# Attention's results turned by VectorE in squares of 32 instead of by TensorE, with the division on GpSimd

## What is computed

```python
Q = (q_in @ wq + bq).reshape(Bq, Sq, H, HD)
Kp = (k_in @ wk + bk).reshape(Bq, Sk, H, HD)
V = (v_in @ wv + bv).reshape(Bq, Sk, H, HD)
scores = jnp.einsum('bqhd,bkhd->bhqk', Q, Kp) / jnp.sqrt(jnp.float32(HD))
# causal: scores above the diagonal are -inf
a = jax.nn.softmax(scores, axis=-1)
o = jnp.einsum('bhqk,bkhd->bqhd', a, V).reshape(Bq, Sq, Dm)
return o @ wo + bo

x = _layernorm(x + _attn(x, x, x, ..., True), ln1_g, ln1_b)
x = _layernorm(x + _attn(x, encoder_output, encoder_output, ..., False), ln2_g, ln2_b)
x = _layernorm(x + _moe(x, ...), ln3_g, ln3_b)
```

## Times and profile before

| | |
|---|---|
| median of 3 runs | 759.5 us (757.66 to 760.63) |
| profiled execution, span | 755.9 us |
| TensorE busy | 711.2 us, 94% |
| TensorE weight load busy | 478.4 us, 63% |
| VectorE busy | 499.0 us, 66% |
| ScalarE busy | 369.2 us, 49% |
| GpSimd busy | 287.3 us, 38% |

### The profile page before, as it was taken

One profiled execution on the slowest core, in us unless ns is written; L12 is line 12 of the kernel. 1 busy time (PEld: TensorE's weight loads), 2 busy tenths in 40 slices (PEclk: granted clock), 3 DMA queues, 4 the chain that ended last, 5 costly groups with the idle time before them and its releaser, 6 DMA issues.

```text
span 755.9 us, 14560 instructions
## 1 busy us (share of the span) xinstructions
PE 711.2 (94%) x4969; PEld 478.4 (63%) x4969; DVE 499.0 (66%) x1376; ACT 369.2 (49%) x749; POOL 287.3 (38%) x558
## 2 busy tenths in 40 slices
PE   6889999999999999999997889999999999999983
PEld 4444434545464454645563666898999999999941
DVE  5679788678766877756687744365666665666436
ACT  4325475665666676677753436433433332332403
POOL 8305521542653463624654333212332332232114
PEclk9999999999999999999997989999999999999997
DMA  8954431343164021316037762676999999999754
GB/s 273 291 145 128 114 98 46 84 129 128 34 179 127 13 60 48 92 43 179 14 113 237 223 210 95 204 262 226 357 328 343 343 326 341 343 332 333 236 187 163
DMA packets 95154, 140.29 MB, mean 186 GB/s; under 512 B 11855, under 2 KB 81077, under 8 KB 92597
## 3 DMA queue, kind: packets, MB, share of 16 engines
q1 hardware_dynamic: 76357, 107.86, 45.5%
q10 hardware_dynamic: 15072, 22.02, 9.1%
q0 software_dynamic: 3648, 9.45, 3.5%
HBM read 110.65 MB, written 28.65 MB: 184 GB/s over the span
## 4 chain that ended last, share of the span: by engine, by line
PE 75%; issue 8%; DVE 7%; DMA 5%; POOL 2%; ACT 1%; SPq 0%; DVEq 0%; ACTq 0%; POOLq 0%
PE out_acc L984 11%; PE score_pair L961 10%; PE work L932 9%; PE score_pair L855 8%; PE work L849 8%; PE work L906 6%; PE work L855 4%; PE score_pair L849 3%; PE work L1008 3%; DVE neg_part_max L1472 3%; PE work L918 2%; PE work L992 2%; PE work L935 2%; DMA arena<-parts_scratch 1%; PE out_acc L849 1%
## 5 line engine op out<-in xcount | busy, mean ns | idle before, releaser
L1472 DVE TENSOR_REDUCE neg_part_max<-work 128x1 f32<-128x512 f32 (+4 forms) x368 | 213.3, 625 | 70.4 <-PE work L935 35.9
L1244 ACT ACTIVATE arena<-score_pair 128x1024 f32<-128x1024 f32 (+2 forms) x224 | 178.9, 839 | 79.8 <-PE score_pair L961 78.9
L932 PE MATMUL work<-arena 96*128 96x77 bf16 (+4 forms) x640 | 118.5, 278 | 10.3 <-ACT arena L1207 2.7
L961 PE MATMUL score_pair<-arena 99*128 99x512 bf16 (+2 forms) x448 | 104.2, 337 | 4.0 <-DMA arena<-negmax_scratch 3.0
L984 PE MATMUL out_acc<-arena 128*32 128x512 f32 (+4 forms) x896 | 103.7, 517 | 2.6 <-DVE arena L1492 2.6
L1904 POOL DMA_INDIRECT chosen_scratch<-arena,scatter_rows x36 | 35.6, 989 | 176.5 <-DVE arena L1404 176.2
L855 PE MATMUL score_pair<-arena 128*128 128x256 f32 x432 | 97.6, 380 | 0.0
L932 PEld LDWEIGHTS work<-arena 96*128 96x128 bf16 x640 | 49.5, 99 | 74.5 <-issue 31.0
L1960 POOL TENSOR_SCALAR_AFFINE_SELECT arena<-arena 128x256 f32<-128x256 f32 x128 | 51.5, 410 | 117.9 <-ACT arena L1244 116.7
L1177 ACT ACTIVATE arena<-work,expert_b_cols 128x128 f32<-128x128 f32 x180 | 51.1, 369 | 77.3 <-PE work L849 64.0
L849 PE MATMUL work<-arena 128*128 128x128 f32 x720 | 87.7, 279 | 0.3 <-issue 0.3
(11 more groups left out here) (257 smaller groups left out, 955.0 us busy)
## 6 DMA issues: line engine op xcount, KB each, us to landing
arena<-in_L_xattn_e_w SPq DMA_DIRECT2D x54, 1024.0 KB, 7.1
arena<-parts_scratch SPq DMA_DIRECT2D x24, 768.0 KB, 6.1
arena<-in_L_xattn_e_w ACTq DMA_DIRECT2D x18, 1024.0 KB, 6.4
parts_scratch<-arena_more SPq DMA_DIRECT2D x24, 384.0 KB, 2.6
parts_scratch<-arena_more SPq DMA_DIRECT2D x24, 256.0 KB, 3.0
parts_scratch<-arena_more SPq DMA_DIRECT2D x24, 128.0 KB, 2.9
residual<-in_x SPq DMA_DIRECT2D x4, 512.0 KB, 8.1
tokens_scratch<-residual SPq DMA_DIRECT2D x2, 1024.0 KB, 5.4
```

The source lines that it names most:

```text
L932: m = pe.matmul(bank[:, j * it.w:(j + 1) * it.w], qa[st.half(it.g)][0:R_S, h, n0:n0 + P], k, start=True, stop=not it.last)
L961: m = pe.matmul(st2[pair][0:rows, j, 0:w], k, qa[st.half(it.g)][0:R_M, h, skip:QG], start=True, stop=True)
L1244: act_e.activation(pt[buf][0:rows, :, 0:w], st2[pair][0:rows, :, 0:w], ACT.Exp, scale=float(HD) ** -0.5).then_inc(pair_taken[pair], 1)
L1472: dve.tensor_reduce(pm[:, it.at, it.t, it.h0:it.h0 + it.nh], bank[:, 0:it.nh * it.w].rearrange("p (j k) -> p j k", j=it.nh), AX.X, ALU.max ...
```

## The change

The two turns on TensorE go. `normalise` is now always VectorE's: it turns `out_acc` in squares of 32x32 while it takes it out of PSUM. A head fills exactly one row of squares, so queries come to lie on partitions (32 of them, for each of 16 squares along the row) and the 32 values of a head along the row, its sum at place 16. VectorE takes the reciprocal of the 16 sums of each partition; `divide` is GpSimd's, a multiplication in SBUF. The quads now hold heads 0, 2, 4, 6 and 1, 3, 5, 7, and the second quad's 16 values are written beside the first quad's, in place of its ones. The new item `merge` (letter `t`) turns the 128x512 result back in squares, into `oT`, which has features on partitions and queries along the row, as `out_tile` needs it as stationary operand. `ot` has three buffers, `onT` is gone, `onat` becomes `oT`. `divide` and `out_turn` take no bank of `work` any more. In `ORDER` only `d` and `t` move: `d` stands close behind its `u` (before, several maxima lay between), `t` a few items behind the second `d` of a group, and the out_tiles stand in a row. All other letters keep their order. Three semaphores come new, three are joined with others.

```diff
-BANKED = ("xt", "ctx", "columns", "proj", "v", "v_bias", "max", "lay", "divide", "out_turn", "out_tile",
+BANKED = ("xt", "ctx", "columns", "proj", "v", "v_bias", "max", "lay", "out_tile",
@@ attend
         steps += [Item(kind, st=st, g=g, quad=quad) for kind in ("normalise", "divide")]
+        if quad == HH // QUAD - 1:
+            steps.append(Item("merge", st=st, g=g))
@@ ORDER, a stretch of self-attention and the end of the last stage
-    "upf2mlq2m3fmwqf2qfm3wqm3wfqsfm3gpdwmyrm2prslm5ruq2dm2qwm3q2m2wmqmqm3qmwmq2sfsm3fwqmqfm2wm2q2fwmqm2f2wfq2fm2q"
+    "lq2m3fmwqf2qfm3wqm3wfqsfm3gpwmyrm2prslm5ruqdqmtmqwm3q2m2wmqmqm3qmwmq2sfsm3fwqmqfm2wm2q2fwmqm2f2wfq2fm2qmwuqdm2qmw"
...
-    "udpdA3rpt2NADWsrNA2lU2so2lt2n3NBn4onUBhVYyUnonNZn3qnqnenha3U2YyR2wuZMaMq2dYR2qwAuq2M2AHNAwudqUwuUd2PZtNtotot"
-    "o2eU2YaZa3zNUYR2LRLRUZNKLSLCHUYPKSTUZNU2YUZUEOIA3XDY2Z2W"
+    "qMRMHyo2qzwuvdPKo2qSewuqdqFtq2BXwuadwax2Oa2xBkxIupdA2tArpNADWsrNA2lU2so2ln3NBn4onUBhVYyUnonNZn3qnqnenha3U2YyR2wuZd"
+    "MaMq2YR2qwAuqdqMtMAHNAwuqdUwuUdPZtNo4eU2YaZa3zNUYR2LRLRUZNKLSLCHUYPKSTUZNU2YUZUEOIA3XDY2Z2W"
@@ buffers
-        ot = [cut("arena", QG) for _ in range(2)]
+        ot = [cut("arena", QG) for _ in range(3)]
-        onat = [a.rearrange("p (t n) -> p t n", t=TB) for a in onat_words]
+        oT = [a.rearrange("p (c t) -> p c t", c=KC) for a in onat_words]
@@ where a quad is laid: the first of a group in ot[0] or ot[1], the second in ot[2]
+        def by_queries(it):
+            whole = ot[place_of[it.st.n, it.g]] if it.quad == 0 else ot[2]
+            return whole.rearrange("p (n v) -> p n v", v=SQUARE)
@@ tensor
-                        h = it.quad * QUAD + it.pair * 2 + j
+                        h = 2 * (it.pair * 2 + j) + it.quad
...
-                elif it.kind == "divide":
-                    e.wait_ge(o_taken, it.n + 1)
-                    o = ot[it.n % 2]
-                    for q in range(QT):
-                        m = pe.transpose(bank[:, q * P:(q + 1) * P], o[:, q * P:(q + 1) * P], ident[:, :])
-                    m.then_inc(full[it.bank], 1)
-
-                elif it.kind == "out_turn":
-                    last = divided[it.b, it.cross, it.t // QT]
-                    e.wait_ge(taken[last.bank], last.use)
-                    for c in range(KC):
-                        m = pe.transpose(bank[:, c * P:(c + 1) * P], onat[it.b][:, it.t, c * P:(c + 1) * P],
-                                         ident[:, :])
-                    m.then_inc(full[it.bank], 1)
-
                 elif it.kind == "out_tile":
-                    o = turned[it.cross, it.b, it.t]
-                    e.wait_ge(taken[o.bank], o.use)
+                    for n in stage_of[it.cross, it.b]:
+                        e.wait_ge(merged, merge_of[n, it.t // QT].n + 1)
@@ scalar: its half of normalise and its copy for out_turn go
-                    act_e.copy(ot[it.n % 2], o_ps[:, :]).then_inc(o_taken, 1)
...
-                    act_e.copy((onT if it.kind == "out_turn" else rT)[it.n % 2],
+                    act_e.copy(rT[it.n % 2],
@@ vector
-                elif it.kind == "normalise" and (it.g + it.quad) % 2 == 0:
+                elif it.kind == "normalise":
                     buf, use = prob_use(weigh_last[it.n], 1)
                     e.wait_ge(prob_taken[buf], use)
...
-                    dve.tensor_copy(ot[it.n % 2], o_ps[:, :]).then_inc(o_taken, 1)
...
+                    elif second_before[it.n]:
+                        e.wait_ge(divided, second_before[it.n].n + 1)
+                    dve.transpose(by_queries(it).rearrange("p n v -> p (n v)"), o_ps[:, :]).then_inc(o_taken, 1)
                     if it.n >= 2:
+                        e.wait_ge(divided, it.n - 1)
+                    e.wait_ge(o_taken, it.n + 1)
+                    dve.reciprocal(rsum[:, it.n % 2], by_queries(it)[:, :, HD]).then_inc(recip_ok, 1)
+
+                elif it.kind == "merge":
+                    for quad in range(HH // QUAD):
+                        e.wait_ge(divided, divide_of[st.n, it.g, quad].n + 1)
...
+                    dve.transpose(oT[st.b][:, st.hh, it.g * QG:(it.g + 1) * QG],
+                                  ot[place_of[st.n, it.g]]).then_inc(merged, 1)
@@ gpsimd
+                elif it.kind == "divide":
+                    e.wait_ge(recip_ok, it.n + 1)
+                    first = ot[place_of[st.n, it.g]].rearrange("p (n v) -> p n v", v=SQUARE)
+                    pool.tensor_tensor(first[:, :, it.quad * HD:(it.quad + 1) * HD], by_queries(it)[:, :, 0:HD],
+                                      rsum[:, it.n % 2].rearrange("p (n o) -> p n o", o=1).to_broadcast(
+                                          [P, QG // SQUARE, HD]), ALU.mult).then_inc(divided, 1)
```

More of the change, by code:

```diff
@@ L210, in project_out @@
     t0 = half * QT
-    tiles = [Item("out_turn", b=b, t=t0, cross=cross)]
-    for t in range(t0, t0 + QT):
-        if t + 1 < t0 + QT:
-            tiles.append(Item("out_turn", b=b, t=t + 1, cross=cross))
-        tiles.append(Item("out_tile", b=b, t=t, cross=cross))
+    tiles = [Item("out_tile", b=b, t=t, cross=cross) for t in range(t0, t0 + QT)]
     return tiles + [Item("out_scale", b=b, cross=cross, g=half)]
@@ L565, in build @@
         divides = find("divide")
-        turned = {(it.cross, it.b, it.t): it for it in find("out_turn")}
+        merges = find("merge")
+        merge_of = {(it.st.n, it.g): it for it in merges}
         tiled = find("out_tile")
@@ L577, in build @@
             pv_end_of_half[it.st.n, it.g] = it
-        for it in divides:
-            divided[it.st.b, it.st.cross, it.g] = it
-        out_read = {turned[it.cross, it.b, it.t].n: it for it in tiled}
+        tile_of = {(it.cross, it.b, it.t): it for it in tiled}
+        divide_of = {(it.st.n, it.g, it.quad): it for it in divides}
         r_turned = {(it.b, it.t): it for it in find("r_turn")}
@@ L584, in build @@
         ended = find("normalise")
+        place_of, merge_before, free, used_by = {}, {}, [0, 1], {}
+        for it in plan:
+            if it.kind == "normalise" and it.quad == 0:
+                a = place_of[it.st.n, it.g] = free.pop(0)
+                merge_before[it.st.n, it.g] = used_by.get(a)
+                used_by[a] = merge_of[it.st.n, it.g]
+            elif it.kind == "merge":
+                free.append(place_of[it.st.n, it.g])
+        second_before = {}
+        for n, it in enumerate([it for it in ended if it.quad == 1]):
+            second_before[it.n] = [z for z in ended if z.quad == 1][n - 1] if n else None
         weigh_last = [it for it in weighs if it.kb == it.st.blocks(it.g) - 1]
         stage_cross = {it.st.n: it.st.cross for it in weighs}
+        stage_of = {(c, b): sorted({it.st.n for it in weighs if (it.st.cross, it.st.b) == (c, b)})
+                    for c in (False, True) for b in range(B)}
         lays = find("lay")
@@ L739, in turn_read @@
         def turn_read(it):
-            it = (out_read if it.kind == "out_turn" else r_read)[it.n - 2]
+            it = r_read[it.n - 2]
             return (logit_sum, it.t % QT + 1) if it.kind == "r_mul_last" else (full[it.bank], it.use)
@@ L1245, in scalar @@
                                      scale=float(HD) ** -0.5).then_inc(pair_taken[pair], 1)
-                elif it.kind == "normalise" and (it.g + it.quad) % 2:
-                    buf, use = prob_use(weigh_last[it.n], 1)
-                    e.wait_ge(prob_taken[buf], use)
-                    if it.n >= 2:
-                        e.wait_ge(full[divides[it.n - 2].bank], divides[it.n - 2].use)
-                    else:
-                        e.wait_ge(full[columns.bank], columns.use)
-                        for z in ctx_of:
-                            e.wait_ge(full[z.bank], z.use)
-                    act_e.copy(ot[it.n % 2], o_ps[:, :]).then_inc(o_taken, 1)
-                elif it.kind in ("out_turn", "r_turn"):
+                elif it.kind == "r_turn":
                     e.wait_ge(full[it.bank], it.use)
@@ L1491, in vector @@
                             e.wait_ge(full[z.bank], z.use)
[L1492 to L1501 removed]
+                    elif second_before[it.n]:
+                        e.wait_ge(divided, second_before[it.n].n + 1)
+                    dve.transpose(by_queries(it).rearrange("p n v -> p (n v)"), o_ps[:, :]).then_inc(o_taken, 1)
+                    if it.n >= 2:
+                        e.wait_ge(divided, it.n - 1)
+                    e.wait_ge(o_taken, it.n + 1)
+                    dve.reciprocal(rsum[:, it.n % 2], by_queries(it)[:, :, HD]).then_inc(recip_ok, 1)
+                elif it.kind == "merge":
+                    for quad in range(HH // QUAD):
+                        e.wait_ge(divided, divide_of[st.n, it.g, quad].n + 1)
                     if st.cross:
[L1503 removed]
+                        z = tile_of[False, st.b, it.g * QT + QT - 1]
                         e.wait_ge(full[z.bank], z.use)
@@ L1610, in vector @@
                     if it.b == 0:
[L1612 removed]
```

(1 more changed line is left out.)

69 lines of the change are left out of this document (26 added, 43 removed), and 2 rows, old and new, of the table KINDS_OF_WORK.

## The result

The changed kernel takes 775.6 us (774.4 to 778.5), the kernel before, run beside it, 759.4 (757.7 to 760.6): a ratio of 1.0248, interval 1.0212 to 1.0283. (The quotient of the two medians alone is 1.0213, the lower end of that interval, so the loss is 16 to 19 us.) The prediction said 745.5, with 757 as its upper end. The profiled execution of the changed kernel has a span of 772.7 us, 16.8 more than before.

The account below looks back on a forecast made before the run. TensorE was taken to bound the kernel from 100 to 400 us. Gain 17.6 - 1 - 3 = 13.6, rounded to 14: span 755.9 to 742, plus 3.6 around it, 745.5 us; range 736 to 757.

Parts of the forecast that it names:

- the first rival: No new wait reaches TensorE and freed banks give back 3 us: gain 21, to 739, or 24, to 736; chance 0.15.
- the turn costs what the copy does: On VectorE, a 128x512 turn out of PSUM was priced at 0.70 us, by the 0.686 us copy.
- the price of the turns from 100 to 300 us: TensorE's removed divide and out_turn turns in that stretch: 7.0 us on the path, by the chain of waits.
- The third: VectorE's turn out of PSUM costs 1.63 us instead of 0.70, so the kernel is slower, 775 us; chance 0.07.
- The second: VectorE sets the pace: waiting merges delay maxima, TensorE waits for banks; 1 us per merge, gain about 2, 757.5; chance 0.15.
- new wait (b): VectorE's merge waits for GpSimd's second product, maxima and TensorE's banks behind it: 3 us for 16 merges, bounds 0 and 16.
- The cover: Where GpSimd has rests or out_scale steps, VectorE's merge waits 2 to 3 us; TensorE's banks and scores cover the larger half.
- Its own tests of this step: VectorE idle ahead of merges under 10 us; out_tile and weigh waits under 4; weight loads' waits for maxima about 16.
- The 17.6 us: Gain on the path from removing TensorE's turns: 7.0 + 7.6 + 3 + 0, out of 23.7 us of issue time.
- the 7.6 from 300 to 400 us: TensorE's removed turns there: 8.6 us by the chain of waits, two divides inside a transfer not counted, leaving 7.6.
- The 3 us from 400 to 483 us: TensorE's 7 divides and 8 out_turns there, 5.4 us: 4 counted on the path, 1 taken off for VectorE's added work.
- Wait (a): All 32 out_acc emptyings queue on VectorE behind maxima, and TensorE's first weigh waits: 1 us for the 16 new ones.

Follow-up runs that it names:

- Late merges: Changed kernel with 14 of its 16 merges moved up to eight items later in the order: 765.2 us, ratio 1.0119 against the kernel before.
- the product's move: Changed kernel with the 32 products on VectorE instead of GpSimd, at the same item of the order: 758.3 us, ratio 1.0007 against the kernel before.
- fewer turns: Kernel before with 128 of TensorE's 192 turns left out, result not the layer's, for timing only: 752.4 us, ratio 0.9952.
- the run: Kernel before with all 32 emptyings of out_acc on VectorE, 16 copies coming from ScalarE: 759.6 us, ratio 1.0041.
- the best version: Changed kernel with the product on VectorE and the merges up to eight items later: 752.7 us, ratio 0.9940 against the kernel before.
- extra turns: Kernel before with 128 of 192 turns left out, plus 20 identity turns ahead of r_mul and out_tile items, 382 to 391 us: 751.8 us, ratio 0.9934.

## Why the prediction was wrong, step by step

*Right:* that the cover isn't complete (the first rival); that the turn costs what the copy does; that VectorE's load is not the bound; the price of the turns from 100 to 300 us, 7.0 predicted, 7.0 when doubled. The product was priced too high, 0.75 us for 0.62, and the text's comparison of 0.734 on GpSimd with 0.424 on VectorE set operands of different kinds side by side: from SBUF VectorE needs 0.59.

*The rivals.* The third, the slow turn, gave 775 us, and 775.6 was measured, but that is chance: the turn takes 0.71 us, not 1.63. The second comes nearest in its mechanism. It said that each merge that waits delays the maxima and that TensorE then waits for banks, which is what happened; only its price, 1 us for each merge, was too low, and its name, VectorE's pace, is wrong, since 19 us more work on VectorE came with 17 us less time.

*The step that failed most is new wait (b),* 3 us for the 16 merges, with an upper bound of 16. Late merges, the order in GpSimd's queue and the product's move show together that this step cost 23 us, over its bound. Three things were mis-sized in it:

- The cover. "TensorE's banks and scores cover the larger half" of a wait of 2 to 3 us. At 160 us the merge waited 3.73 us. A weigh, a score and one more maximum covered 1.7 us of that, less than half. And the wait of TensorE doesn't end with the wait of VectorE: the merge and the first maximum came first, 1.35 us more. So TensorE stood for 3.35 us.
- What follows a wait. The text counted the idle time, not the lower clock behind it. One such place made a stair of 4.8 us, where the text allowed it about 1. In the time of the whole kernel it was worth 4.3 us by the ratios, but their intervals overlap by a tenth of a per cent, and the profiled spans differ by 1.5 us; that the stair itself goes is shown, how much of it reaches the end is not.
- The other direction. The text asked who waits behind VectorE at the merge, and didn't ask who waits behind GpSimd at the product. That queue holds rests, whose results go through scratch to TensorE. Moving five products behind them gave 4.4 us by the medians, 3.6 by the ratios.

Together: 775.6 to 765.2 by late merges, to 760.8 by the order in GpSimd's queue; late merges with the product moved off GpSimd reach 752.7. The hand-over in both directions and the places of the merges cost 23 us, where the prediction had 3. Its own tests of this step gave the alarm: idle time ahead of the merge was to stay under 10 us and was 15.8, waits of weigh and out_tile for turn and merge under 4 together and those of weigh alone were 10.4, the waits of weight loads for the maxima not much over 16 and were 23.9.

*The second failure is the gain itself.* The 17.6 us were the price of having the turns on the path; leaving out 128 of 192 gave 3.6 us, by proportion 5.4 for all. The part from 100 to 300 us holds roughly (3.4 of 4.7). The failing term is the 7.6 from 300 to 400 us: from 306 to 404 us fewer turns gave 0.5 instead of 5.1. Doubled, the turns cost 5.6 there. A likely reason, not shown piece by piece: the chain's share for L992 and L999 was time that TensorE spent on them while other things were due soon anyway, and a share of the chain tells what the chain went through, not what is left when that piece is gone. The 3 us from 400 to 483 us did not show either: the 4.7 us by which the lag of fewer turns falls from 404 to 472 us are about what the trace of the kernel before lost itself, and the 3.9 us by which it had got ahead from 94 to 404 us are already all that the times show.

*Wait (a)* was 1 us in the text and 3 us in the run. By these terms a kernel without the hand-over should stand at 756.4 - 5.4 + 3 = 754, and the best version was measured at 752.7. The 23 us are the difference between the changed kernel and that one, so they are no check of their own.

*Open:* why the gain of the fewer turns is so small between 306 and 404 us. To 367 us they gained 1.7 us, from 367 to 391 us they lost 1.2 of it again. The granted clock is 0.64 from 382 to 386 us, but with extra turns and a clock of 1.00 there 0.9 us were lost all the same, and the time didn't change, within what 0.2% can tell. How (b) divides between the waits, the lower clock behind them and the places of the merges is open too. Nor have I located all of the 5.6 us that late merges gave with the product on VectorE; 1.2 of them are there at 94 us.

## What to carry to other kernels

When a step is handed to an idle engine and comes back, price three queues, not one duration: what stands ahead of it on the helper, what stands behind the engine that waits for it, and what stands behind the helper while it waits for its input. Here 32 products of 0.6 us each made the kernel 17 us slower on GpSimd, which had time to spare, than on the busier VectorE, because each engine works its queue in order and a hand-over waits for two queues. Test a gain in both directions: that doubling a piece costs 16 us doesn't mean that removing it gives them. And before a table of differences is read, look whether all its columns move together: then it is the reference that moved.

## What the runs showed of the hardware

The turn of squares of 128x512 fp32 takes 711 ns out of PSUM and 706 ns within SBUF, within 4% of the copy of the same size. The product with a broadcast operand, both from SBUF, takes 623 ns on GpSimd and 591 to 605 on VectorE; from PSUM VectorE took 424. The Trainium skill, "GPSIMD Engine Reference", 4.1 Engine selection, has GpSimd about twice as slow with two inputs; in these rows it is 3 to 5% slower, so the cost of the move lay in the waits and not in the speed.

TensorE's granted clock, 1.00 before, read 0.77 over the 15 us that held a wait of 3.35 us, and the same matmuls took 0.61 instead of 0.38 us and 1.94 instead of 1.06 behind it. It fell also with no wait over 1 us: 0.76, then 0.50, from 382 us on, where TensorE was busy 3.21 and 3.17 of 4 us. With 20 turns put there it stayed at 1.00.
